# Slot arithmetic on GpSimd, scatters spread anew, and turned sums copied before the normalised rows, in a one-core Mamba-2 and mixture-of-experts kernel

## The chip, the core and the metric

The kernel runs on one core of a Trainium2 chip. The metric is the device time of one execution in microseconds (us); the kernel before has a median of 817.68 us over three runs (816.87 to 819.04). Engines are named as in the profile: PE is TensorE (PEld its weight loads), DVE is VectorE, ACT is ScalarE, POOL is GpSimd, SP is SyncE, which here only issues DMAs.

## The reference

16 sequences of 512 tokens with 128 channels pass through a Mamba-2 block and then through a top-2 mixture of 8 experts, each followed by a residual sum and a layer norm. Cut to what matters here:

```python
# block 1: projections, causal convolution of 4 taps, silu, state-space scan, gated RMS norm, output projection
h = dA_t * h + dt_t * x_t (outer) B_t ;  y = C_t . h + D * x_t
x = layernorm(x + (y * rsqrt(mean(y*y) + eps) * norm_w * silu(z)) @ Wout.T)
# block 2: router and experts
gates = sigmoid(u @ centroids.T)
topk_vals, topk_idx = top_k(gates, 2)
gates = mask(topk_vals) / sum(mask)
out = sum_e gates[e] * (gelu(u @ W1[e] + b1[e]) @ W2[e] + b2[e])
x = layernorm(x + out)
```

## The kernel before, in words

**First phase (about 0 to 478 us).** One slot of work per sequence, 16 in all, written out one after another. Sequence n is scanned in slot n, in four chunks of 128 tokens (c = 0 to 3). In the same slot sequence q = n + 1 is projected and convolved, sequence r = n - 1 is normalised and routed, and the rows of sequence n - 2 are scattered, sorted by expert, into a table in HBM (`sorted_rows`). Each engine has its own instruction list in a fixed order; semaphores tie them together. An instruction that waits holds back everything behind it on its engine. Nothing is scheduled at run time, so the order is the order of the code.

The names that matter:

- PE, chunk c: exponents of the next chunk (`exponents`, L420 to L425, into the bank `pl`), transposes of the chunk (L518, L520), product with the carried state (L524), a projection of q (L399), at c = 1 the turned sums of q (L412, `turn_parts`, into the bank `p4`), the masked product (L542), the carried part (L548), and the state product (L556), which needs `Xdd` from POOL and `Btok` from ACT. At the end of chunk 1 the rows of r are transposed (L566) into the same bank `p4`, so that this waits both until ACT has normalised the rows (`u_ready`) and until ACT has copied the turned sums out of it (`S_ready`).
- ACT, chunk 1: it normalises the four row blocks of r (L810), applies the first tap (L730, `acc`), copies the decays of q (L719, `cur`), copies the turned sums (L725, `S`, `keep_parts`), and then squares `yv` (L783). `uT` (L822) is the copy of the transposed rows.
- DVE: `Gm` (L1076) opens each slot. `take_ranks` (L1005 to L1009) reads the ranks of sequence n - 2 out of PSUM at the end of chunk 0. `place_rows` (L1017 to L1027) at the end of chunk 1 works out the row number of each token's two copies (`slot`), and writes their weight and token number into the last two columns of `rowA` and `rowB`.
- POOL: `Xdd` (L1379) and `decayed` (L1373) for the scan, `gt` (L1359, the gated output, once a chunk), two powers (`rstd` L1394, `rms` L1415), and eight indirect DMAs (L1366) which scatter the rows of sequence n - 2: A0 and A1 behind `gt` of chunk 1, A2 and A3 behind that of chunk 2, and B0 to B3 behind `rms` at the slot's end. The first instruction of the next slot on POOL is `Xdd` of its chunk 0, which so stands behind all four B scatters.

After slot 15 comes a tail: sequence 15 is normalised and routed, and POOL scatters sequences 14 and 15 (eight DMAs each), while DVE works out a table of 136 tiles.

**Second phase (about 478 to 770 us).** 136 tiles of 128 sorted rows go through the experts. **Third phase (to 815 us).** The two expert outputs of each token are added and normalised. Neither is touched by the change, except that they start when the last scatter has landed.

Of the kernel before, what the change touches and what calls it, by code (L numbers as in the profile page):

```python
# [52 lines left out]
POS_STEPS = 4  # L53
# [24 lines left out]
def build(nc, t, out):  # L78
    ctx = ExitStack()
    with ctx:  # L80
# [6 lines left out]
        def sem(name):  # L87
# [31 lines left out]
        token_id = sb("token_id", [P, NC])  # L119
# [42 lines left out]
        rowA = [sb(f"rowA{i}", [P, NC, ROW]) for i in range(2)]  # L162
        rowB = [sb(f"rowB{i}", [P, NC, ROW]) for i in range(2)]
# [11 lines left out]
        slotf = sb("slotf", [P, NC, 2])  # L175
# [34 lines left out]
              for big in (acc, xc[0]) for i in range(2)]  # L210
# [40 lines left out]
                     "slot_ready", "parts_ready", "split_step")  # L251
        (x1_ready, Gm_ready, M_ready, Xdt_ready, v_ready, yv_ready, state_ready, sp_step, a_ready,
         tap_done, conv_done, carried_ready, ln_step, ve_ready, shift_ready, u_ready, gate_step, chosen_ready,
         ms_ready, pos_step, rank_read, slot_ready, parts_ready, split_step) = [sem(n) for n in names_dve]
        names_pool = ("picks_made", "Xdd_ready", "decayed_ready", "g_ready", "rms_ready", "rstd_ready")
        (picks_made, Xdd_ready, decayed_ready, g_ready, rms_ready, rstd_ready) = [sem(n) for n in names_pool]
# [136 lines left out]
        def _(pe):  # L393
# [106 lines left out]
            def slot_pe(s, scan, project, route):  # L500
# [4 lines left out]
                for c in range(NC):  # L505
                    tok = slice(c * P, (c + 1) * P)
                    n = NC * s.n + c
                    if scan and (c + 1 < NC or project):
                        if not route and c == 0:
                            pe.wait_ge(v_ready, 2)  # L510
                        exponents(s if c + 1 < NC else q, (c + 1) % NC)
# [23 lines left out]
                    if scan:  # L535
# [140 lines left out]
        def _(act):  # L676
# [109 lines left out]
            def slot_act(s, scan, project, route):  # L786
# [4 lines left out]
                for c in range(NC):  # L791
# [94 lines left out]
        def _(dve):  # L886
# [124 lines left out]

            def place_rows(r):

                link = chain(pos_step, POS_STEPS * r.n + 1)
                dve.wait_ge(rank_read, r.n + 1)
                dve.wait_ge(rowB_ready, r.n + 1)
                dve.reciprocal(gsum[:, :], gsum[:, :])  # L1017
                link(dve.tensor_tensor(prow[:, :, :, :], picks[:, :, :, :],
                                       rows[:, :, :].unsqueeze(2).broadcast_to([P, NC, 2, E]), ALU.mult))
                link(dve.tensor_reduce(slotf[:, :, :], prow[:, :, :, :], AX_X, ALU.add))  # L1020
                for row, k in ((rowA, 0), (rowB, 1)):
                    dve.scalar_tensor_tensor(out=row[r.par][:, :, P + 1], in0=top[:, :, k], scalar=2.0,
                                             in1=gsum[:, :], op0=ALU.mult, op1=ALU.mult)
                    dve.tensor_scalar(row[r.par][:, :, P].bitcast(I32), token_id[:, :],
                                      float(TOKENS * k), None, ALU.add)
                link(dve.tensor_copy(slot[r.par][:, :, :], slotf[:, :, :]))
                dve.tensor_scalar(token_id[:, :], token_id[:, :], float(TOKS), None,  # L1027
                                  ALU.add).then_inc(slot_ready, 1)
# [27 lines left out]
            def slot_dve(s, scan, project, route):  # L1056
# [24 lines left out]
                for c in range(NC):  # L1081
# [50 lines left out]
                    if c == 1 and not (isinstance(s.n, int) and s.n < 2):  # L1132
                        place_rows(s.plus(-2))
# [9 lines left out]
                if route:  # L1143
# [4 lines left out]
                    wait_apart(dve, gate_step, gate + 2)  # L1148
                    for k in range(NC):
# [349 lines left out]
```

## Time and profile before

| | |
|---|---|
| median of three runs | 817.68 us (816.87 to 819.04) |
| the profiled execution | 816.69 us, of which the span is 814.9 us |
| busy in the span | PE 667.5, DVE 617.5, ACT 475.8, POOL 433.0 us |
| granted clock of PE in slots 1 to 15 | 1.00, full speed |

The page gives busy time by engine, then the span in 40 slices. The first 22 slices are the slots, with PE and DVE both at 8 to 9 tenths. PE busy counts modelled ends of pipelined matmuls, so two engines near 9 tenths say only that both are candidates; which of them waits for which is read from the chain of waits and from the timelines of single engines.

### The profile page before, as it was taken

What the parts mean: (1) busy time and instruction counts of PE and PEld (TensorE: products, weight loads), DVE (VectorE), ACT (ScalarE), POOL (GpSimd) and SP (SyncE); (2) the same over time, 40 slices, a digit from 0 to 9 for tenths busy, and PEclk for the clock granted to TensorE, in tenths of its full rate; (3) what the DMA queues carried; (4) which work ended last, traced back from release to release, by engine and by line L of the source; (5) the groups of instructions that cost most, each with busy time, mean ns of one, the idle gap of its engine ahead of it and who ended that gap; (6) DMA issues with size and microseconds to landing.
All of it is one profiled execution on the core that took longest, in us unless ns stands there. A gap on an engine that the chain in (4) does not pass through costs nothing.

```text
span 814.9 us, 21092 instructions
## 1 busy us (share of the span) xinstructions
PE 667.5 (82%) x5092; PEld 546.9 (67%) x5093; DVE 617.5 (76%) x2128; ACT 475.8 (58%) x1179; POOL 433.0 (53%) x498
## 2 busy tenths in 40 slices
PE   7969999888898898988987139999999999999300
PEld 5846666566665566655665129999999999999300
DVE  4398989889999899998896536666667666667485
ACT  3737766676766767667673115555555555556165
POOL 4023265656656566565756634555555555555464
PEclk9999999999999999999999559999999999999755
DMA  9160010111101111011100122222222222222496
GB/s 258 33 229 14 15 41 14 37 30 40 41 14 37 31 40 37 18 33 34 41 20 24 57 60 57 66 63 65 64 65 65 65 63 64 65 64 70 108 311 203
DMA packets 74801, 54.09 MB, mean 66 GB/s; under 512 B 9435, under 2 KB 70110, under 8 KB 74480
## 3 DMA queue, kind: packets, MB, share of 16 engines
q1 hardware_dynamic: 56400, 31.90, 14.9%
q0 software_dynamic: 8448, 16.93, 6.3%
q10 hardware_dynamic: 9888, 4.49, 2.0%
q8 instruction: 29, 0.48, 0.3%
q14 instruction: 36, 0.29, 0.1%
HBM read 31.11 MB, written 22.69 MB: 66 GB/s over the span
## 4 chain that ended last, share of the span: by engine, by line
PE 71%; issue 9%; ACT 7%; DVE 5%; POOL 3%; DMA 2%; ACTq 1%; SPq 1%; DVEq 0%; POOLq 0%
PE pl L633 16%; PE p L645 14%; PE pj L399 5%; PE p L585 4%; PE p L593 3%; PE p L542 3%; PE p L548 2%; PE pj L627 2%; ACT rowA L810 2%; ACT sz L872 2%; POOL sorted_rows L1366 2%; PE pj L407 2%; PE p L556 2%; PE p L496 2%; PE p L407 2%
## 5 line engine op out<-in xcount | busy, mean ns | idle before, releaser
L851 ACT ACTIVATE L<-pl,b_sb 128x128 f32<-128x128 f32 x544 | 155.4, 369 | 118.1 <-PE pl L633 118.1
L1428 POOL DMA_INDIRECT moe_rows<-yv,xs x136 | 145.7, 1072 | 140.5 <-DVE yv L1235 124.1
L633 PE MATMUL pl<-Btok,M 128*128 128x128 f32 x1088 | 151.7, 283 | 1.2 <-DVE M L1223 0.7
L924 DVE SCALAR_TENSOR_TENSOR acc<-pj,conv_w_sb,acc 128x511 f32<-128x511 f32 (+2 forms) x192 | 142.7, 743 | 4.0 <-ACT acc L730 1.1
L645 PE MATMUL p<-w,L 128*128 x1088 | 143.9, 275 | 1.3 <-ACT L L851 1.3
L633 PEld LDWEIGHTS pl<-Btok,M 128*128 128x128 f32 x1088 | 133.7, 193 | 4.3 <-DVE M L1223 1.4
L645 PEld LDWEIGHTS p<-w,L 128*128 128x128 f32 x1088 | 132.4, 192 | 1.8 <-issue 1.8
L1219 DVE COPY Btok<-pj 128x128 f32<-128x128 f32 x136 | 39.7, 292 | 78.2 <-PE pl L633 63.2
L1379 POOL TENSOR_TENSOR Xdd<-Xdt,cur 128x256 f32<-128x256 f32 x48 | 29.5, 615 | 88.0 <-DVE Xdt L1091 80.1
L1366 POOL DMA_INDIRECT sorted_rows<-rowA,slot x64 | 64.7, 1011 | 19.1 <-issue 17.0
L1366 POOL DMA_INDIRECT sorted_rows<-rowB,slot x64 | 62.7, 980 | 18.0 <-issue 18.0
L730 ACT ACTIVATE acc<-pj,conv_b_sb,conv_w_sb 128x512 f32<-128x512 f32 x64 | 49.5, 773 | 35.4 <-PE pj L399 35.3
L399 PE MATMUL pj<-xT,w_xbc 128*128 128x512 f32 x128 | 66.5, 601 | 0.0
L542 PEld LDWEIGHTS p<-M,Xdt 128*64 128x64 f32 x512 | 27.3, 136 | 52.5 <-issue 48.9
L627 PE MATMUL pj<-ident,xs 128*128 128x128 f32 x136 | 39.9, 294 | 23.3 <-DMA xs<-sorted_rows 20.8
L1223 DVE COPY M<-w 128x512 f32 x136 | 57.0, 419 | 0.0
L688 ACT ACTIVATE pl<-pl 128x512 f32<-128x512 f32 x64 | 37.3, 582 | 33.8 <-PE pl L425 33.2
L1359 POOL TENSOR_TENSOR gt<-yv,sz 128x256 f32<-128x256 f32 x64 | 47.0, 734 | 11.3 <-DVE yv L1117 10.6
L1235 DVE SCALAR_TENSOR_TENSOR yv<-yv,xs 128x128 f32<-128x128 f32 x136 | 47.8, 352 | 4.8
L1232 DVE TENSOR_TENSOR yv<-p,b2e_mem 128x128 f32<-128x128 f32 x136 | 39.5, 291 | 15.2 <-PE p L645 8.9
L542 PE MATMUL p<-M,Xdt 128*64 128x128 f32 x512 | 42.1, 284 | 9.5 <-issue 6.8
L998 DVE TENSOR_TENSOR M<-pl,Gm 128x512 f32<-128x512 f32 x64 | 43.8, 685 | 2.0 <-ACT pl L688 1.4
(204 smaller groups left out, 1341.7 us busy)
## 6 DMA issues: line engine op xcount, KB each, us to landing
xs<-sorted_rows SPq DMA_DIRECT2D x136, 65.0 KB, 1.8
xres<-in_x SPq DMA_DIRECT2D x16, 256.0 KB
w<-in_w SPq DMA_DIRECT2D x2, 2048.0 KB, 10.2
acc<-moe_rows SPq DMA_DIRECT2D x16, 256.0 KB, 4.2
xc<-moe_rows SPq DMA_DIRECT2D x16, 256.0 KB, 5.0
out<-sz ACTq DMA_DIRECT2D x16, 256.0 KB, 4.6
moe_rows<-yv,xs POOLq DMA_INDIRECT x136, 2.4
xc<-in_x SPq DMA_DIRECT2D x4, 256.0 KB, 5.1
```

Source lines behind the costliest of these rows:

```text
L399: pe.matmul(pj[k % 2][:, :], w_xbc[:, k * P:(k + 1) * P], xT[:, q.n, :], start=True, stop=True).then_inc(proj_psum, 1)
L542: mm = pe.matmul(p7[half, (h // 2) * P:(h // 2 + 1) * P], Xdt[c % 2][:, h * HD:(h + 1) * HD], M[c % 2][:, h, :], start=(h < 2), stop=(c == ...
L627: pe.transpose(pj[k % 2][:, 0:P], xs[k][:, 0:P], ident[:, :]).then_inc(sT_psum, 1)
L633: mm = pe.matmul(pl[k % 2][:, f * P:(f + 1) * P], w1e[k % 2][:, f * P:(f + 1) * P], sT[k % 2][:, :], start=True, stop=True)
L645: mm = pe.matmul(o[:, 0:P], hT[k % 2][:, f, :], w2[:, bass.ds(e, 1), f, :].rearrange("p e d -> p (e d)"), start=(f == 0), stop=(f == FB - 1))
L730: act.activation(acc[:, c, :], pj[c % 2][:, :], ACT.Identity, bias=conv_b[:, c:c + 1], scale=conv_w[:, c, TAPS - 1:TAPS]).then_inc(tap0_do ...
L851: act.activation(hT[k % 2][:, f, :], pl[k % 2][:, f * P:(f + 1) * P], ACT.Gelu, bias=b1[:, bass.ds(e * FB + f, 1)]).then_inc(hT_ready, 1)
L924: ins = dve.scalar_tensor_tensor(out=acc[:, k, j:TOKS], in0=pj[k % 2][:, 0:TOKS - j], scalar=conv_w[:, k, TAPS - 1 - j:TAPS - j], in1=acc[ ...
L1223: dve.tensor_copy(w1e[k % 2], w1[:, bass.ds(e, 1), :].rearrange("p e f -> p (e f)")).then_inc(w1e_ready, 1)
L1235: dve.scalar_tensor_tensor(out=ye[k % 4], in0=ye[k % 4], scalar=xs[k][:, P + 1:P + 2], in1=xs[k][:, 0:P], op0=ALU.mult, op1=ALU.add).then_ ...
L1366: pool.indirect_dma_start(out=sorted_rows[:, :], out_offset=bass.IndirectOffsetOnAxis(slot[q.par][:, c, k:k + 1], 0), in_=(rowA, rowB)[k][ ...
L1428: pool.indirect_dma_start(out=moe_rows[:, :], out_offset=bass.IndirectOffsetOnAxis(xs[k][:, P:P + 1].bitcast(I32), 0), in_=ye[k % 4], in_o ...
```

## The change

`place_rows` leaves DVE and is written again for POOL, for both copies of a row at once. `rowA` and `rowB` become the two halves of one tile `pair`, and `token_id` gets two sets of columns. The sum over the eight experts, one `tensor_reduce` on DVE, becomes three halving additions. The reciprocal of the gate sum stays on DVE, in `take_ranks`. On POOL the arithmetic stands behind `gt` of chunk 0. The eight scatters are laid out anew: A0 ahead of `Xdd` of chunk 2, A1 to A3 behind `gt` of chunk 1, B0 behind that of chunk 2, and B1 to B3 behind `rms`. On ACT the copy of the turned sums goes ahead of the normalising, and the copy of the decays goes to chunk 3. On PE the exponents of chunk 2 are issued ahead of the state product of chunk 0 and no longer at the start of chunk 1.

```diff
@@ take_ranks (DVE)
                 dve.wait_ge(rank_psum, r.n + 1)
+                wait(dve, slot_ready, r.n)
 ...
                 dve.tensor_tensor(next_row[:, :], p4[:, NC * E:(NC + 1) * E], next_row[:, :],
                                   ALU.add).then_inc(rank_read, 1)
+                dve.reciprocal(gsum[:, :], gsum[:, :]).then_inc(rows_ready, 1)
-            def place_rows(r):     (DVE, ten instructions, L1013 to L1028)
@@ slot_pe
-                    if scan and (c + 1 < NC or project):
+                    if scan and c != 1 and (c + 1 < NC or project):
 ...
                             pe.wait_ge(Btok_ready, (NC - 1) * s.n + c + 1)
                             pe.wait_ge(Xdd_ready, (NC - 1) * s.n + c + 1)
                             if c == 0:
+                                exponents(s, 2)
                                 pe.wait_ge(sz_ready, CC * (s.n + 1))
@@ slot_act
+                    if project and c == 1:
+                        keep_parts(q, p4[0:KS, 0:P])
                     if route and c == 1:
 ...
-                    if project and c == 1:
+                    if project and c == 3:
                         set_current(q)
-                        keep_parts(q, p4[0:KS, 0:P])
@@ gpsimd
+            def place_rows(r):
+                done = [PLACE_STEPS * r.n]
+                def link(ins):
+                    done[0] += 1
+                    ins.then_inc(place_step, 1)
+                    pool.wait_ge(place_step, done[0])
+                pool.wait_ge(rows_ready, r.n + 1)
+                wait(pool, slot_ready, r.n)
+                pool.wait_ge(rowB_ready, r.n + 1)
+                pool.tensor_tensor(gain[:, :], gsum[:, :], gsum[:, :], ALU.add)
+                link(pool.tensor_tensor(prow[:, :, :, :], picks[:, :, :, :],
+                                        rows[:, :, :].unsqueeze(2).broadcast_to([P, NC, 2, E]), ALU.mult))
+                part = prow
+                for k in range(3):
+                    w = E >> (k + 1)
+                    if k == 1:
+                        pool.tensor_tensor(pair[r.par][:, :, :, P + 1], top[:, :, 0:2].rearrange("p c k -> p k c"),
+                                           gain[:, :].unsqueeze(1).broadcast_to([P, 2, NC]), ALU.mult)
+                    if k == 2:
+                        pool.tensor_copy(pair[r.par][:, :, :, P].bitcast(I32), token_id[:, :, :])
+                    link(pool.tensor_tensor(half[k][:, :, :, :], part[:, :, :, 0:w], part[:, :, :, w:2 * w],
+                                            ALU.add))
+                    part = half[k]
+                link(pool.tensor_copy(slot[r.par][:, :, :], half[2][:, :, :, 0]))
+                pool.tensor_scalar(token_id[:, :, :], token_id[:, :, :], 1.0, float(TOKS), ALU.mult,
+                                   ALU.add).then_inc(slot_ready, 1)
```

On POOL, from the first instruction of a slot to the first of the next, with the kernel before (the names are those of the list above; `sorted_rows<-rowA` is a scatter of A):

```order
L1379 TENSOR_TENSOR Xdd<-Xdt,cur 128x256
L1394 TENSOR_TENSOR rstd<-ve,neg_half 128x4
L1373 TENSOR_TENSOR decayed<-state,cur 128x256
L1379 TENSOR_TENSOR Xdd<-Xdt,cur 128x256
L1359 TENSOR_TENSOR gt<-yv,sz 128x2x128
L1373 TENSOR_TENSOR decayed<-state,cur 128x256
L1379 TENSOR_TENSOR Xdd<-Xdt,cur 128x256
L1359 TENSOR_TENSOR gt<-yv,sz 128x2x128
L1366 DMA sorted_rows<-rowA,slot 67584x130 x2
L1359 TENSOR_TENSOR gt<-yv,sz 128x2x128
L1366 DMA sorted_rows<-rowA,slot 67584x130 x2
L1359 TENSOR_TENSOR gt<-yv,sz 128x2x128
```

And with the changed kernel, from the first `gt` of a slot on to the first instruction of the next:

```order
L1345 TENSOR_TENSOR gt<-yv,sz 128x2x128
L1360 TENSOR_TENSOR gain<-gsum 128x4
L1361 TENSOR_TENSOR prow<-picks,rows 128x64
L1371 TENSOR_TENSOR half<-prow 128x32
L1367 TENSOR_TENSOR pair<-top,gain 128x8
L1371 TENSOR_TENSOR half<-half 128x16
L1370 CAST pair<-token_id 128x8
L1371 TENSOR_TENSOR half<-half 128x8
L1374 CAST slot<-half 128x8
L1375 TENSOR_SCALAR token_id<-token_id 128x8
L1389 TENSOR_TENSOR decayed<-state,cur 128x256
L1382 DMA sorted_rows<-pair,slot 67584x130
```

Nine small instructions and one scatter now stand between `gt` of chunk 0 and `Xdd` of chunk 2, and three scatters, where there were four, between `rms` and the next slot.

On ACT, chunk 1 of a slot before, from the normalising to the copy of the transposed rows:

```order
L810 ACTIVATE rowA<-rowA,shift,rstd 128x128 x4
L730 ACTIVATE acc<-pj,conv_b_sb,conv_w_sb 128x512
L719 COPY cur<-vals 128x80
L725 CAST S<-p 96x128
L783 ACTIVATE ysq<-yv 128x2x128
L822 COPY uT<-p 128x512
```

And the same place now:

```order
L729 CAST S<-p 96x128
L816 ACTIVATE pair<-pair,shift,rstd 128x128 x4
L734 ACTIVATE acc<-pj,conv_b_sb,conv_w_sb 128x512
L787 ACTIVATE ysq<-yv 128x2x128
L827 COPY uT<-p 128x512
```

The copy `S` no longer stands behind the normalising and a tap, and `cur` is gone from this chunk.

On PE, chunk 0 and the head of chunk 1 now:

```order
L545 MATMUL p<-M,Xdt 64x128 x4
L423 MATMUL pl<-too_early,ident_b 128x512
L425 MATMUL pl<-pick_s,S 128x512
L428 MATMUL pl<-S,pick_t 128x128 x4
L560 MATMUL p<-Xdd,Btok 128x256
L521 MATMUL p<-ident,xc 128x128 x2
```

Before, the three rows of exponents stood behind the state product; both orders have them behind PE's wait for `Xdd`.

## Rows read from the trace of the kernel before

**Rows 1.** Busy time by engine in one steady slot (stretch, length, busy, clock).

```profile
288.00:314.00 26.00, 23.10 (x164) 15.93 (x162) 23.54 (x77) 17.53 (x35) 16.25 (x20) 1.00 0.11 33
```

**Rows 2.** The chain that ended last: start us, us, engine, tile, line, count.

```profile
299.43 1.32 issue
...
304.54 1.25 ACT rowA L810 x3
305.78 0.66 ACT acc L730
306.45 0.15 ACT cur L719
306.60 0.17 ACT S L725
306.76 0.14 issue
306.90 0.63 PE p L566 x4
...
323.42 0.86 PE pj L399 x2
```

**Rows 3.** Timeline of PE in the same slot, the state product of chunk 2.

```profile
310.88 0.60 PE L556 MATMUL p<-Xdd,Btok 128*128 128x256 f32 x2
```

**Rows 4.** Timeline of POOL in that slot: start us, us, what, [idle before].

```profile
299.04 0.96 POOL L1366 DMA_INDIRECT sorted_rows<-rowB,slot  x1 [0.30 <-issue]
300.03 0.62 POOL L1379 TENSOR_TENSOR Xdd<-Xdt,cur 128x256 f32<-128x256 f32 x1
...
304.04 0.73 POOL L1359 TENSOR_TENSOR gt<-yv,sz 128x256 f32<-128x256 f32 x1
...
309.58 0.61 POOL L1379 TENSOR_TENSOR Xdd<-Xdt,cur 128x256 f32<-128x256 f32 x1 [2.09 <-DVE Xdt L1091]
```

**Rows 5.** Timeline of DVE in that slot.

```profile
301.45 0.42 DVE L1122 COPY state<-p 128x256 f32<-128x256 f32 x1 [0.34 <-PE p L556]
...
303.63 0.46 DVE L1103 SCALAR_TENSOR_TENSOR shift<-mv,rstd 128x4 f32<-128x4 f32 x1
...
306.71 0.17 DVE L1017 RECIPROCAL gsum<-gsum 128x4 f32<-128x4 f32 x1
...
307.92 0.74 DVE L924 SCALAR_TENSOR_TENSOR acc<-pj,conv_w_sb,acc 128x511 f32<-128x511 f32 x1
```

**Rows 6.** Timeline of ACT in that slot, the copy of the transposed rows.

```profile
307.62 0.59 ACT L822 COPY uT<-p 128x512 f32<-128x512 f32 x1 [0.55 <-PE p L566]
```

**Rows 7.** All 16 `Gm` (min/median/max ns, first and last start), then those opening slots 2, 3.

```profile
L1076 DVE TENSOR_TENSOR Gm<-p,upto x16: 677/681/691, 38.5 to 424.9; 128x512 f32<-128x512 f32 x16
...
92.24 0.68 DVE L1076 TENSOR_TENSOR Gm<-p,upto 128x512 f32<-128x512 f32 x1
...
116.98 0.68 DVE L1076 TENSOR_TENSOR Gm<-p,upto 128x512 f32<-128x512 f32 x1
```

**Rows 8.** Timeline of POOL at the start, two small additions, the second waiting for the first.

```profile
6.19 0.21 POOL L1347 TENSOR_TENSOR which<-ident 96x16 f32<-96x16 f32 x1
6.48 0.22 POOL L1348 TENSOR_TENSOR which<-which,ident 96x16 f32<-96x16 f32 x1
```

**Rows 9.** The small `shift` on DVE: ns min/median/max over all slots.

```profile
L1103 DVE SCALAR_TENSOR_TENSOR shift<-mv,rstd x16: 161/463/465, 73.8 to 452.4; 128x4 f32<-128x4 f32 x16
```

**Rows 10.** Timelines of DVE and POOL in the tail.

```profile
449.66 0.32 DVE L1054 TENSOR_SCALAR ve<-mv 128x4 f32<-128x4 f32 x1
...
450.32 0.96 POOL L1366 DMA_INDIRECT sorted_rows<-rowB,slot  x1 [0.30 <-issue]
451.31 1.04 POOL L1394 TENSOR_TENSOR rstd<-ve,neg_half 128x4 f32<-128x4 f32 x1
454.49 1.03 POOL L1366 DMA_INDIRECT sorted_rows<-rowA,slot  x1 [2.14 <-DVE token_id L1027]
...
466.34 1.92 POOL L1366 DMA_INDIRECT sorted_rows<-rowA,slot  x1 [0.31 <-issue]
...
473.03 0.40 DVE L1207 CAST table<-tval 1x136 int32<-1x136 f32 x1
```

More of the change, by code:

```diff
@@ L52 @@
 NH = NC * H
-POS_STEPS = 4
+POS_STEPS = 1
+PLACE_STEPS = 5
 FIN_STEPS = 3
@@ L118, in build @@
         iota_tile = sb("iota_tile", [P, TILES])
-        token_id = sb("token_id", [P, NC])
+        token_id = sb("token_id", [P, 2, NC])
         region = sb("region", [P, E])
@@ L161, in build @@
         shift = sb("shift", [P, NC])
-        rowA = [sb(f"rowA{i}", [P, NC, ROW]) for i in range(2)]
-        rowB = [sb(f"rowB{i}", [P, NC, ROW]) for i in range(2)]
+        pair = [sb(f"pair{i}", [P, 2, NC, ROW]) for i in range(2)]
+        rowA = [b[:, 0] for b in pair]
+        rowB = [b[:, 1] for b in pair]
         uT = sb("uT", [P, TOKS])
@@ L174, in build @@
         prow = sb("prow", [P, NC, 2, E])
-        slotf = sb("slotf", [P, NC, 2])
+        half = [sb(f"half{i}", [P, NC, 2, E >> (i + 1)]) for i in range(3)]
+        gain = sb("gain", [P, NC])
         slot = [sb(f"slot{i}", [P, NC, 2], I32) for i in range(2)]
@@ L1010, in take_ranks @@
                                   ALU.add).then_inc(rank_read, 1)
[L1012 to L1028, printed above, removed]
+                dve.reciprocal(gsum[:, :], gsum[:, :]).then_inc(rows_ready, 1)
             def residual(s):
@@ L1131, in slot_dve @@
                         take_ranks(s.plus(-2))
-                    if c == 1 and not (isinstance(s.n, int) and s.n < 2):
-                        place_rows(s.plus(-2))
                 gate = GATE_STEPS * (r.n if route else 0)
@@ L1148, in slot_dve @@
                     wait_apart(dve, gate_step, gate + 2)
+                    wait(dve, slot_ready, r.n)
                     for k in range(NC):
@@ L1164, in slot_dve @@
                     link(dve.tensor_copy(topf[:, :, :], topi[:, :, 0:2]))
-                    wait(dve, slot_ready, r.n)
                     link(dve.tensor_tensor(
@@ L1175, in _ @@
             take_ranks(Seq(0, SEQS - 1))
-            place_rows(Seq(0, SEQS - 1))
             link = chain(table_step, 0)
@@ L1333, in _ @@
                            allow_small_or_imprecise_dtypes=True))
-            step(pool.iota(token_id[:, :], pattern=[[P, NC]], base=0, channel_multiplier=1,
+            step(pool.iota(token_id[:, :, :], pattern=[[TOKENS, 2], [P, NC]], base=0, channel_multiplier=1,
                            allow_small_or_imprecise_dtypes=True))
@@ L1398, in slot_pool @@
                     gate_y(s, 0)
+                if scatters:
+                    place_rows(old)
+                if scan:
                     decay_state(s, 2)
+                if scatters:
+                    scatter(old, 0, 0)
+                if scan:
                     decay_x(s, 2)
@@ L1402, in slot_pool @@
                 if scatters:
-                    scatter(old, 0, 0)
-                    scatter(old, 1, 0)
+                    for c in range(1, NC):
+                        scatter(old, c, 0)
                 if scan:
@@ L1407, in slot_pool @@
                 if scatters:
-                    scatter(old, 2, 0)
-                    scatter(old, 3, 0)
+                    scatter(old, 0, 1)
                 if scan:
@@ L1416, in slot_pool @@
                 if scatters:
-                    for c in range(NC):
+                    for c in range(1, NC):
                         scatter(old, c, 1)
             slots(pool, slot_pool)
+            place_rows(Seq(0, SEQS - 1))
             for k in range(2):
```

8 lines of the change are left out of this document (4 added, 4 removed).

## The prediction, made before the changed kernel had run

> **What bounds the kernel now.** I read first the busy time by stage, then the chain of waits through one steady slot, then the timelines of POOL, DVE and ACT beside it. In a steady slot PE is busy 23.1 and DVE 23.5 of 26 us, at a full granted clock [rows 1], so neither alone is the bound; the reader is to see that both have about 2.5 us to give and to ask which wait ends last. The chain answers: from 306.90 to past 323.42 it is PE without a gap, and before that it leaves PE twice [rows 2]. First PE stands 1.32 us behind its masked product until the state product of chunk 0. POOL explains that: `Xdd`, which the product needs, starts at 300.03, the moment the last of four B scatters ends [rows 4]. Second, the chain goes from the normalising on ACT through a tap, the `cur` copy and the `S` copy to the transposes at 306.90 [rows 2]. The transposes need the normalised rows, done at 305.78, but the copy `S` lets them go only 0.98 us later (0.66 + 0.15 + 0.17). The slots are regular: `Gm` of slot 3 starts at 116.98 and that of slot 15 at 424.9, twelve periods of 25.66 us; slot 2, which has no B scatters ahead of it, lasts 116.98 - 92.24 = 24.74 us [rows 7].
>
> **The `S` copy ahead of the normalising.** It takes 0.98 us out of the way to the transposes in every slot that both routes and projects: 1 to 14, fourteen. What is late next is the `uT` copy, which waited 0.55 us for those transposes [rows 6]; ACT reaches it 0.32 us earlier, since `cur` and `S` are gone ahead of it, so it can follow by 0.87, and the rest is taken up by PE, whose queue from there to the slot's end is full. I take 0.98, with 0.86 as the low end. 14 x 0.98 = 13.7 us. `cur` goes to chunk 3, beside PE work, and is needed only in the next slot: nothing. The price is a wait: ACT's normalising is now queued behind PE's turned sums. Estimate: the state ends at 301.5, then half a microsecond for the product with it, 0.86 for the projection [rows 2], 0.2 for the turn and 0.26 for the copy make 303.3, and `shift` ends at 303.6. So this costs nothing, but it is the thinnest margin on ACT.
>
> **One B scatter fewer behind `rms`.** A scatter costs POOL 1.26 us (0.96 and the 0.30 ahead of it, [rows 4]). `Xdd` could then start at 298.77, about when its input is there, and PE's 1.32 us go, less what the exponents do there: they are 0.66 us and move ahead of the state product, which is work that PE did just behind it, so the sum on PE is the same and the exponents reach ACT earlier. But PE is not alone there. DVE waited only 0.34 us for the state [rows 5]; from there its queue is full up to `shift`, on which ACT waits. So the slot gains what `shift` gains: 0.34, at most 0.50 with small waits behind it, less 0.09 for the added reciprocal. I take 0.40 in slots 3 to 14 (12 x 0.40 = 4.8) and 0.4 in slot 15, together 5.2 us. Ends: 0.25, and 0.92, the difference between the steady period and slot 2 [rows 7], which also holds an earlier start.
>
> **The arithmetic off DVE.** It took 307.92 - 306.71 = 1.21 us a slot [rows 5]. It lies behind `shift` and ahead of the wait of DVE for chunk 2, so it is not on the chain. I cost its removal at nothing: it only keeps DVE from becoming the bound once PE moves up by 1.4 us.
>
> **The arithmetic on POOL.** Nine instructions, five of them waited for. A 96x16 addition with a wait costs 6.48 - 6.19 = 0.29 us from start to start [rows 8]. Five x 0.29 = 1.43, 0.08 more for the 64 elements of the first product (0.62 us for 256 elements, [rows 4], is 1.7 ns an element), and four unwaited ones at about 0.15: 2.1 us. Ends: 1.2 us, DVE's price, and 9 x 0.62 = 5.6 us, the row of the large product. I take 2.1, nearest to the rows of like size. What lies behind it: `decayed` and A0, then `Xdd` of chunk 2, for which PE comes at 310.88 [rows 3], or about 309.4 with the gains above. `gt` ends at 304.77 - 0.45 = 304.3; then 2.1, a short wait for the state, 0.6 for `decayed`, 1.2 for A0 and 0.6 for `Xdd` make 309.2. So there is room for an arithmetic of about 2.5 us; each microsecond beyond it costs one in every slot from 2 on. Behind chunk 2 POOL issues four scatters up to the last `gt`, as before.
>
> The Trainium skill speaks against this step: GPSIMD Engine Reference, Engine selection, gives two-input elementwise work to VectorE, since GpSimd is about twice as slow. By that rule an estimate would be 2 x 1.21 = 2.4 us, still within the 2.5; no run so far shows these instructions on POOL, and the sum would stay the same by either.
>
> **The tail.** With three B scatters `rstd` waits no longer for POOL but for `ve`, whose row ends at 449.98: 450.1 instead of 451.31 [rows 10]. The 2.14 us in which POOL then waited for DVE's arithmetic become 2.2 us of its own, so A0 comes 1.15 us earlier. But the arithmetic for sequence 15, which DVE did beside the eight scatters, now stands between them and the next eight (466.34): 2.1 + 0.17 - 0.3 = 1.9. Net 0.8 us slower, with the gains of the slots in front. The 16 scatters themselves stay. DVE's tile table, whose last row ends at 473.43 [rows 10], starts when that arithmetic is done, some 4 us later, and is ready at 477.4; eight scatters of 1.26 behind the ninth's place at 467.1 end after that and must land first, so the table stays covered.
>
> **Sum.** 13.7 + 5.2 - 0.8 = 18.1 us off the profiled execution of 816.69, whose span is 814.9: 798.6. The median of the runs shown is 0.99 above it; from 817.68 it gives 799.6, and I say 799.5. The second and third phase are untouched. With both low ends it is 14 x 0.86 + 13 x 0.25 - 0.8 = 14.5 off, 803; with the state product's high end 13 x 0.52 more, 793. A difference under 0.3% (2.5 us) can't be told from none here.
>
> **Rivals.** (1) The arithmetic on POOL takes 2.6 to 3.7 us, say 3.1. For it: short rows and strides of 130 elements that no row of before shows. Against: the same engine's small rows at 0.21. Then 0.6 us of each of 13 slots goes back, and 2 x 1.0 in the tail: 10 less, 809.5.
> (2) Slower: POOL's small instructions are held up by DVE. `shift`, a 128x4 instruction, takes 0.161 us in the tail and 0.463 in the slots, beside POOL's work [rows 9]: the two hold each other up by 0.30. If each of the nine is held so, the arithmetic is 2.1 + 2.7 = 4.8 us, 2.3 beyond the room, against a gain of 1.38 a slot: 0.9 lost in each of 12 slots, about 1.3 in slot 2, 1 in slot 15, 0.8 + 5.4 in the tail, less 1 in slot 1: 18 us slower, 836. It decides from an arithmetic of 3.7 us on, price and room together. Against it: DVE's work in that stretch is taps, `yv` and state sums that read PSUM, and POOL's large products cost the same in every slot. That the two share their way to SBUF stands also in the Trainium skill, GPSIMD Engine Reference, Specifications, for DVE instructions with two SBUF inputs; the rows of `shift` agree, and by that rule the taps with their one SBUF input would not hold POOL.
> (3) The copy `S` becomes the wait: the turned sums come later than `shift`, and normalising starts 0.5 us late. For it: 0.3 us of margin. Against: PE is ahead there, as its 1.32 us are gone. 18.1 - 14 x 0.5 = 11 off, 806.5.
> (4) Nothing moves since DVE is full in truth: 817. Against: DVE did wait, 0.34 us for the state [rows 5].
>
> **How the numbers follow.** Forecast 0.70, (1) 0.12, (2) 0.08, (3) 0.07, (4) 0.03. The forecast's own range is 793 to 803; with (1) and (3) the range reaches 793.5 to 811, and leaves out (2), (4) and a rest. Faster: 0.70 + 0.12 + 0.07 less a little for a long arithmetic, 0.87; same 0.04; slower 0.09.
>
> **What would show it.** A period between two `Gm` of 24.2 to 24.4 us; the state product of chunk 0 within 0.2 us of the masked product, not counting the exponents; the transposes of rows waiting for `rowA` and no longer for `S`, some 0.45 us behind the state product of chunk 1; nine POOL instructions from the first `gt` in 2.0 to 2.4 us; in the tail, 2.1 us of arithmetic between the eighth and ninth scatter. The prediction is wrong if the state product of chunk 2 waits for `Xdd`, if the arithmetic is over 2.5 us, or if `shift` has not moved up in the slot.

## The result, and the profile after

The changed kernel took 797.24 us (median of 4, 795.83 to 798.2) against 817.27 us of the kernel before beside it: a ratio of 0.9751, 95% interval 0.9728 to 0.9773. Forecast were 799.5 us and a range of 793.5 to 811. The profiled execution took 798.2 us.

I read it in the order of the prediction. First the `Gm` that open the slots: all of them (min/median/max ns, first and last start), then two single ones (start us, us).

```profile
L1065 DVE TENSOR_TENSOR Gm<-p,upto x16: 679/681/692, 38.0 to 404.1; 128x512 f32<-128x512 f32 x16
...
91.51 0.68 DVE L1065 TENSOR_TENSOR Gm<-p,upto 128x512 f32<-128x512 f32 x1
...
115.40 0.68 DVE L1065 TENSOR_TENSOR Gm<-p,upto 128x512 f32<-128x512 f32 x1
```

The period is (404.1 - 115.4) / 12 = 24.06 us against 25.66 [rows 7]: 1.60 us less in each of twelve slots. Slot 2 lasts 23.89 against 24.74, and slot 1, where no B scatter lies behind `rms` either, has lost the same 0.85. Busy time in a steady slot (stretch, length, busy of PE, weight load, DVE, ACT, POOL, clock, DMA share, GB/s):

```profile
284.00:308.00 24.00, 22.91 (x162) 15.90 (x161) 21.99 (x68) 17.41 (x34) 17.77 (x28) 1.00 0.11 34
```

PE does nearly the same work in 24 us instead of 26 [rows 1]. The two stretches are not the same share of a period, so I take DVE and POOL over slots 3 to 14 as a whole: DVE is busy 263.5 us instead of 278.6 and POOL 213.1 instead of 190.5, that is 1.3 us less and 1.9 us more a slot. The timeline of PE in the slot whose `Gm` starts at 283.86 (start us, us, what, [idle before]):

```profile
286.32 0.66 PE L545 MATMUL p<-M,Xdt 128*64 128x128 f32 x8
287.02 0.38 PE L423 MATMUL pl<-too_early,ident_b 128*128 128x512 bf16 x1
...
287.68 0.65 PE L560 MATMUL p<-Xdd,Btok 128*128 128x256 f32 x2
...
289.05 0.70 PE L527 MATMUL p<-state,xc 128*128 128x256 f32 x2 [0.40 <-DVE state L1111]
...
291.73 0.60 PE L560 MATMUL p<-Xdd,Btok 128*128 128x256 f32 x2
292.87 0.66 PE L570 MATMUL p<-ident,pair 128*128 128x128 f32 x4 [0.54 <-ACT pair L816]
```

PE's 1.32 us ahead of the state product of chunk 0 [rows 2] are gone: L560 follows the exponents without a wait. The transposes (L570) now wait for the normalised rows, 0.54 us behind the state product of chunk 1. ACT in the same slot:

```profile
290.70 0.26 ACT L729 CAST S<-p 96x128 bf16<-96x128 f32 x1 [1.74 <-PE p L415]
291.17 1.65 ACT L816 ACTIVATE pair<-pair,shift,rstd 128x128 f32<-128x128 f32 x4 [0.20 <-DVE shift L1092]
...
293.69 0.56 ACT L827 COPY uT<-p 128x512 f32<-128x512 f32 x1
```

The `S` copy stands ahead of the normalising and is done 0.2 us before `shift` comes; the last to come is `shift`. DVE from the state to the third chunk:

```profile
288.58 0.41 DVE L1111 COPY state<-p 128x256 f32<-128x256 f32 x1
...
290.67 0.47 DVE L1092 SCALAR_TENSOR_TENSOR shift<-mv,rstd 128x4 f32<-128x4 f32 x1
...
293.75 0.74 DVE L929 SCALAR_TENSOR_TENSOR acc<-pj,conv_w_sb,acc 128x511 f32<-128x511 f32 x1
295.08 0.42 DVE L1080 TENSOR_TENSOR Xdt<-p,cur 128x256 f32<-128x256 f32 x1 [0.58 <-PE p L523]
```

The state waits for nothing (0.34 before, [rows 5]). `shift` ends 7.28 us behind `Gm` in this slot; in the median of slots 3 to 14 it is 7.35 against 7.86 before, 0.51 earlier. In the same median the transposes start 9.09 us behind `Gm` instead of 10.66, so nearly the whole gain of the slot is made by there. Without the arithmetic DVE waits 0.58 us for chunk 2. POOL:

```profile
285.32 0.96 POOL L1382 DMA_INDIRECT sorted_rows<-pair,slot  x1 [0.30 <-issue]
286.31 0.61 POOL L1395 TENSOR_TENSOR Xdd<-Xdt,cur 128x256 f32<-128x256 f32 x1
...
291.76 0.20 POOL L1360 TENSOR_TENSOR gain<-gsum 128x4 f32<-128x4 f32 x1
291.91 0.33 POOL L1361 TENSOR_TENSOR prow<-picks,rows 128x64 f32<-128x64 f32 x1
292.31 0.25 POOL L1371 TENSOR_TENSOR half<-prow 128x32 f32<-128x32 f32 x1
292.64 0.21 POOL L1367 TENSOR_TENSOR pair<-top,gain 128x8 f32<-128x8 f32 x1
...
293.77 0.19 POOL L1375 TENSOR_SCALAR token_id<-token_id 128x8 f32<-128x8 f32 x1
293.94 0.60 POOL L1389 TENSOR_TENSOR decayed<-state,cur 128x256 f32<-128x256 f32 x1
```

The nine small instructions take 293.94 - 291.76 = 2.18 us. In the tail, behind the last slot:

```profile
428.16 1.04 POOL L1410 TENSOR_TENSOR rstd<-ve,neg_half 128x4 f32<-128x4 f32 x1 [0.16 <-DVE ve L1043]
429.19 0.19 POOL L1360 TENSOR_TENSOR gain<-gsum 128x4 f32<-128x4 f32 x1
...
432.18 1.09 POOL L1382 DMA_INDIRECT sorted_rows<-pair,slot  x1 [0.79 <-POOL token_id L1375]
...
443.76 0.21 POOL L1360 TENSOR_TENSOR gain<-gsum 128x4 f32<-128x4 f32 x1
...
446.75 1.06 POOL L1382 DMA_INDIRECT sorted_rows<-pair,slot  x1 [0.78 <-POOL token_id L1375]
...
456.30 0.95 POOL L1382 DMA_INDIRECT sorted_rows<-pair,slot  x1 [0.30 <-issue]
```

From the last `Gm` to the last scatter's start it is 52.2 us, 0.9 more than the 51.3 before. Of the second and third phase, whose code is the same, I count the time from that start to the end of the span: 796.3 - 456.3 = 340.0, before 338.7.

### The profile page after: what moved, and what is told of

Read it like the earlier page. It is cut to its first block, busy times and chain, and to the rows that moved or that the text cites. A ratio compares the mean times of both kernels' runs of the same rounds, so it can differ in the third digit from the quotient of the medians.

```text
span 796.3 us, 21108 instructions
## 1 busy us (share of the span) xinstructions
PE 673.3 (85%) x5092; PEld 548.5 (69%) x5093; DVE 600.1 (75%) x2000; ACT 473.8 (60%) x1179; POOL 465.2 (58%) x642
## 4 chain that ended last, share of the span: by engine, by line
PE 69%; DVE 9%; issue 8%; POOL 5%; ACT 4%; DMA 3%; DVEq 1%; SPq 0%; ACTq 0%; POOLq 0%
PE pl L637 16%; PE p L649 15%; PE pj L402 4%; PE p L589 4%; PE p L597 3%; POOL sorted_rows L1382 3%; PE p L551 2%; PE pj L631 2%; PE p L545 2%; ACT pair L816 2%; PE pj L410 2%; PE p L499 2%; PE p L527 2%; PE p L410 2%; PE pl L446 2%
## 5 line engine op out<-in xcount | busy, mean ns | idle before, releaser
L1450 POOL DMA_INDIRECT moe_rows<-yv,xs x136 | 147.3, 1083 | 139.4 <-DVE yv L1221 122.0
L1382 POOL DMA_INDIRECT sorted_rows<-pair,slot x128 | 128.3, 1002 | 35.2 <-issue 33.6
L734 ACT ACTIVATE acc<-pj,conv_b_sb,conv_w_sb 128x512 f32<-128x512 f32 x64 | 49.5, 773 | 33.1 <-PE pj L402 33.1
L1080 DVE TENSOR_TENSOR Xdt<-p,cur 128x256 f32<-128x256 f32 x64 | 27.0, 422 | 20.5 <-ACT Btok L802 10.4
```

The source lines that it names most:

```text
L734: act.activation(acc[:, c, :], pj[c % 2][:, :], ACT.Identity, bias=conv_b[:, c:c + 1], scale=conv_w[:, c, TAPS - 1:TAPS]).then_inc(tap0_do ...
L1382: pool.indirect_dma_start(out=sorted_rows[:, :], out_offset=bass.IndirectOffsetOnAxis(slot[q.par][:, c, k:k + 1], 0), in_=(rowA, rowB)[k][ ...
L1450: pool.indirect_dma_start(out=moe_rows[:, :], out_offset=bass.IndirectOffsetOnAxis(xs[k][:, P:P + 1].bitcast(I32), 0), in_=ye[k % 4], in_o ...
```

## The experiments

The theory at this point: a slot hangs on the chain from the state of chunk 0 over `shift`, the normalising and the transposes to the pairs' end; the copies and the scatter each took their own term off it, and DVE's arithmetic lay beside it at no price. The rivals: the gain is DVE's relief, or the exponents' new place. In the table the period is that of slots 3 to 14, "tail" runs from the last `Gm` to the last scatter's start, and the ratio is to the kernel before on the same chip.

| kernel | median us | ratio, 95% | period | tail |
|---|---|---|---|---|
| changed | 797.24 | 0.9751, 0.9728 to 0.9773 | 24.06 | 52.2 |
| e1_copies_back | 811.85 | 0.9932, 0.9915 to 0.9949 | 25.09 | 52.2 |
| e2_four_behind | 813.52 | 0.9954, 0.9936 to 0.9971 | 25.12 | 56.2 |
| e3_exponents_back | 800.7 | 0.9772, 0.975 to 0.9794 | 24.13 | 52.4 |
| e4_dve_load | 806.21 | 0.985, 0.9827 to 0.9874 | 24.69 | 52.5 |
| e5_four_more | 813.57 | 0.9944, 0.9923 to 0.9965 | 25.03 | 55.6 |
| b1_copies_ahead | 810.0 | 0.9893, 0.9868 to 0.9917 | 25.02 | 51.3 |
| b2_three_behind | 813.13 | 0.9922, 0.9898 to 0.9945 | 25.28 | 49.9 |
| b3_both | 806.09 | 0.9836, 0.9812 to 0.9859 | 24.75 | 50.1 |
| t1_tail_on_dve | 791.23 | 0.9698, 0.9684 to 0.9712 | 24.06 | 47.7 |
| v1_shift_early | 793.99 | 0.9726, 0.9708 to 0.9743 | 23.70 | 52.2 |
| v2_all | 790.69 | 0.9681, 0.9667 to 0.9694 | 23.82 | 49.5 |
| v3_early_and_tail | 795.59 | 0.9684, 0.9665 to 0.9703 | 23.94 | 48.0 |

**Undo the copies** (e1, from the changed kernel: `S` and `cur` copied in chunk 1 behind the normalising, as before):

```diff
-                    if project and c == 1:
-                        keep_parts(q, p4[0:KS, 0:P])
...
-                    if project and c == 3:
+                    if project and c == 1:
...
+                        keep_parts(q, p4[0:KS, 0:P])
```

> The changed kernel with ACT's two copies (turned sums, decays) back behind the normalising and the tap of chunk 1. Theory: the copy of the turned sums was on the path to the transposes of the rows; that path takes back 0.86 us (what slots 1 and 2 gained) to 1.07 us in each of 14 slots: 12 to 15 us, so 809 to 812 us, period of a slot 24.9 to 25.1 us, and the transposes wait for S again. Rival (the relief of DVE carries the gain, the copy only filled a gap): at most 3 us slower, about 800.

Measured: 811.85 us, period 25.09, so 1.03 us a slot. PE in the slot whose `Gm` starts at 267.25:

```profile
277.39 0.63 PE L570 MATMUL p<-ident,pair 128*128 128x128 f32 x4 [1.60 <-ACT S L729]
```

And ACT there:

```profile
274.63 1.65 ACT L814 ACTIVATE pair<-pair,shift,rstd 128x128 f32<-128x128 f32 x4 [2.20 <-DVE shift L1091]
...
276.99 0.26 ACT L729 CAST S<-p 96x128 bf16<-96x128 f32 x1
```

The rows are done at 276.28 and `S` at 277.25, and the transposes start right behind `S`: the 0.98 of the prediction, in the place it named.

**Undo the scatter's move** (e2, all four B scatters behind `rms`):

```diff
-                if scatters:
-                    scatter(old, 0, 1)
...
-                    for c in range(1, NC):
+                    for c in range(NC):
```

> The changed kernel with scatter B0 back behind rms, so that four scatters again stand ahead of Xdd of chunk 0. Theory: Xdd comes 1.26 us later, PE waits, and since the exponents now stand between that wait and the state product, the state comes 1.0 us later, shift too, in slots 3 to 15; the tail adds 1.2: 13 to 15 us slower, 810 to 812, period 25.0 to 25.1. Rival (the stall was beside other work, as DVE waited only 0.34 us for it in the kernel before): 4 to 6 us slower, 802.

Measured: 813.52 us, period 25.12 (1.06 a slot); PE of the slot whose `Gm` starts at 265.58:

```profile
270.10 0.38 PE L423 MATMUL pl<-too_early,ident_b 128*128 128x512 bf16 x1 [1.32 <-issue]
...
270.75 0.65 PE L560 MATMUL p<-Xdd,Btok 128*128 128x256 f32 x2
```

PE's 1.32 us are back, now ahead of the exponents that stand there. The state product starts 5.17 us behind `Gm`, 0.66 later than in the kernel before (4.51): the exponents now lie between the wait and the product. That is why undoing this move here costs more than the move alone gives (b2, below). The tail grew by 4.0 us where I expected 1.2; in slot 15, too, everything behind the fourth scatter comes later.

**The exponents alone** (e3, those of chunk 2 back in their old place):

```diff
-                    if scan and c != 1 and (c + 1 < NC or project):
+                    if scan and (c + 1 < NC or project):
...
-                                exponents(s, 2)
```

> The changed kernel with the exponents of chunk 2 back at the start of chunk 1, behind the state product. Theory: PE does the same work in the other order, DVE does not wait for the state either way and ACT has 0.9 us to spare: no change, 796 to 799, period 24.0 to 24.1. Rival (the earlier exponents are what brought shift forward by 0.59 where I had reckoned 0.40): 0.2 us a slot, 3 us slower, 800.

The period is 24.13, 0.07 a slot, and the last scatter starts at 456.1 (456.3 in the changed kernel). So the exponents' place gives next to nothing. The median is 3.5 us higher, but the intervals of the two ratios overlap, and the kernel before took 819.03 us beside this one and 817.27 beside the changed kernel. What shows of the rest lies behind the last scatter: 345.1 us to the end of the span instead of 340.0, in code that is the same. PE there waits once for long:

```profile
710.42 2.08 PE L636 MATMUL pl<-Btok,M 128*128 128x128 f32 x8 [2.28 <-DVE M L1208]
```

b3 below has the same wait, 2.26 us, and 343.1 us behind its last scatter's start. Hence the slots are compared by their periods below, not by the medians.

**Give DVE its load back** (e4: nine small DVE instructions whose results nobody uses, where the arithmetic stood):

```diff
+                for k in range(3):
+                    dve.tensor_scalar(idle_a[:, :], iota_tile[:, 0:8], 1.0, None, ALU.add)
+                    dve.tensor_scalar(idle_b[:, :], iota_tile[:, 0:8], 1.0, None, ALU.add)
+                    link(dve.tensor_scalar(idle_c[:, :], iota_tile[:, 0:64], 1.0, None, ALU.add))
...
+                    if c == 1 and not (isinstance(s.n, int) and s.n < 2):
+                        idle_work(s.n - 2)
```

> The changed kernel with nine added DVE instructions of no use (about 1.2 us, as long as the arithmetic that left DVE) where that arithmetic stood. Theory: DVE waits 0.58 us there for the transposes, so chunk 2's Xdt comes 0.55 us later and its masked product 0.4 us later, in 13 or 14 slots: 5 to 6 us slower, 802 to 803, period 24.4 to 24.5. Rival (DVE became free by the whole 1.2 us, it is the bound): 16 us slower, 813. Rival (the prediction's own cost of nothing): 797.

Measured: 806.21 us, period 24.69. DVE in the slot whose `Gm` starts at 264.43:

```profile
274.39 0.16 DVE L1027 TENSOR_SCALAR idle_a<-iota_tile 128x8 f32<-128x8 f32 x1
...
274.77 0.47 DVE L1027 TENSOR_SCALAR idle_a<-iota_tile 128x8 f32<-128x8 f32 x1
...
275.82 0.75 DVE L933 SCALAR_TENSOR_TENSOR acc<-pj,conv_w_sb,acc 128x511 f32<-128x511 f32 x1
276.49 0.42 DVE L1092 TENSOR_TENSOR Xdt<-p,cur 128x256 f32<-128x256 f32 x1
```

And PE there, the masked product of chunk 2:

```profile
277.01 0.66 PE L549 MATMUL p<-M,Xdt 128*64 128x128 f32 x8 [0.56 <-issue]
```

DVE no longer waits for chunk 2, PE stands 0.56 us ahead of its product until `Xdt` is there, and `Xdt` starts 12.06 us behind `Gm` instead of 11.29. The load is 275.82 - 274.39 = 1.43 us and the slot pays 0.63 of it, more than I expected. The 0.58 us in which the changed kernel's DVE waits here cover the rest, or nearly: 1.43 - 0.58 = 0.85, of which `Xdt` shows 0.77. The load is longer than what had left DVE, which is 1.21 less the 0.09 of the reciprocal, or 1.12 us; so 0.63 is more than the price of the arithmetic itself. But DVE's work at this place is not free.

**More arithmetic on POOL** (e5: four waited-for additions whose result nobody uses, ahead of the step that releases the scatters):

```diff
+                link(pool.tensor_tensor(filler[:, :], gain[:, :], gain[:, :], ALU.add))
...
```

> The changed kernel with four more waited-for 128x4 additions in POOL's arithmetic, about 1.1 us (2.2 becomes 3.3). Theory: there is room for 2.5; beyond it the state product of chunk 2 waits for Xdd: 0.8 us in each of 13 slots and 2.2 in the tail, 12 to 14 us slower, 810, period 24.85. Rival (POOL is off the path): only the tail, 2 us slower, 799.

Measured: 813.57 us, period 25.03. The four cost 1.12 us, 0.28 from start to start. PE in the slot whose `Gm` starts at 267.41:

```profile
281.41 0.67 PE L561 MATMUL p<-Xdd,Btok 128*128 128x256 f32 x2 [0.74 <-POOL Xdd L1400]
```

The state product of chunk 2 now waits for `Xdd`, as rival (1) says of a long arithmetic. Of 1.12 us more the slot pays 0.97, so the room ends at some 2.18 + 0.15 = 2.3 us of arithmetic; I had 2.5. The tail grew by 3.4 us, 1.1 more than twice the four.

**One move alone, in the kernel before** (b1 only the copies, b2 only the scatter, b3 both; the arithmetic stays on DVE and the exponents where they were). The edits:

```diff
+                    if project and c == 1:
+                        keep_parts(q, p4[0:KS, 0:P])
...
+                    scatter(old, 0, 1)
...
-                    for c in range(NC):
+                    for c in range(1, NC):
```

> The kernel before with nothing changed but ACT's two copies: the turned sums ahead of the normalising, the decays in chunk 3. Theory: 0.86 to 0.98 us less in each of 14 slots, 12 to 14 us faster, 803 to 805, period 24.7 to 24.8. Rival (with DVE still carrying the arithmetic it is full and nothing moves): within 3 us of the kernel before.

> The kernel before with nothing changed but scatter B0, issued ahead of the last gt and no longer behind rms. Theory: PE's wait of 1.32 us goes, the slot gains 0.4 to 0.6 (what DVE waited for the state, and its followers) in 12 slots, 0.4 in slot 15 and 1.1 in the tail: 6 to 9 us faster, 808 to 811, period 25.1 to 25.3. Rival (all of PE's 1.32 us is gained): 17 us faster, 800. Rival (gt of chunk 3 and the gated output come later by the scatter's 1.2 us and eat it): no change.

> The kernel before with both moves (copies ahead on ACT, B0 ahead of the last gt), the arithmetic still on DVE and the exponents of chunk 2 in their old place. Theory: the two gains add up, less 0.3 to 0.5 us a slot because DVE's 1.2 us of arithmetic now reach past its wait in chunk 2; period 24.3 to 24.5, and the tail is 3 us shorter than in the changed kernel: 798 to 801, that is within 4 us of the changed kernel. Rival (the move of the arithmetic is what made room, without it DVE is the bound): period 25.1 or more, 810.

Periods: b1 25.02 (0.64 off), b2 25.28 (0.38 off, my 0.40), b3 24.75 (0.91 off). b1 fell short of its 0.98 and b3 of its sum. For b1 the timeline of DVE (`Gm` at 265.82) says why:

```profile
277.42 0.17 DVE L1028 TENSOR_SCALAR token_id<-token_id 128x4 f32<-128x4 f32 x1
277.50 0.74 DVE L925 SCALAR_TENSOR_TENSOR acc<-pj,conv_w_sb,acc 128x511 f32<-128x511 f32 x1
278.16 0.41 DVE L1092 TENSOR_TENSOR Xdt<-p,cur 128x256 f32<-128x256 f32 x1
```

Before, DVE waited 0.42 us ahead of this `Xdt` of chunk 2. In b1 the wait is gone: DVE, full with the arithmetic, sets when chunk 2 starts. Its `Xdt` comes 12.34 us behind `Gm` instead of 12.84 in the kernel before, whatever PE has gained. In b2 DVE still waits 0.42 us there.

Where each gain goes is read from the same instructions of PE in all slots. The table has their starts in us behind `Gm`, medians of slots 3 to 14 ("output" is the product of `gt` with `w_out`, L593 before and L597 now):

| kernel | transposes | masked product, chunk 2 | output | next `Gm` |
|---|---|---|---|---|
| before | 10.66 | 13.51 | 22.33 | 25.61 |
| b1 | 9.60 | 12.86 | 21.69 | 24.97 |
| b2 | 10.16 | 13.00 | 21.92 | 25.25 |
| b3 | 9.08 | 12.34 | 21.40 | 24.73 |
| changed | 9.09 | 11.96 | 20.79 | 24.06 |
| e4 | 9.08 | 12.58 | 21.41 | 24.68 |

With both moves the transposes are as early as in the changed kernel, 1.58 us earlier than before. Then b3 gives back 0.38 at the masked product, where PE waits for DVE's `Xdt`, and 0.23 more at the output, where it waits for the last `gt` on POOL. In b3, in the slot whose `Gm` starts at 264.97, two lines of PE and then one of POOL:

```profile
277.32 0.66 PE L542 MATMUL p<-M,Xdt 128*64 128x128 f32 x8 [0.32 <-issue]
...
286.37 2.05 PE L593 MATMUL p<-w_out,gt 128*128 128x128 f32 x16
...
285.57 0.75 POOL L1360 TENSOR_TENSOR gt<-yv,sz 128x256 f32<-128x256 f32 x1
```

The last `gt` ends at 286.32 and the output starts at 286.37. Between the `gt` of chunk 1 and the last one b3 has five scatters and the changed kernel four, since A0 stands ahead of chunk 2 there. In the changed kernel (`Gm` at 259.73) the last `gt` ends a microsecond ahead of the output:

```profile
278.81 0.73 POOL L1345 TENSOR_TENSOR gt<-yv,sz 128x256 f32<-128x256 f32 x1
...
280.51 1.98 PE L597 MATMUL p<-w_out,gt 128*128 128x128 f32 x16
```

In e4 nothing but DVE's load differs from the changed kernel, and all of its 0.62 arises at the masked product.

**The tail's arithmetic on DVE** (t1: in the changed kernel, for sequences 14 and 15 only, whose arithmetic lies outside the slots):

```diff
+            def place_rows(r):
...
+                link(dve.tensor_reduce(half[0][:, :, :, 0], prow[:, :, :, :], AX_X, ALU.add))
...
+                        if not scan:
+                            place_rows(s.plus(-2))
...
+            place_rows(Seq(0, SEQS - 1))
...
-                if scatters:
+                if scatters and scan:
...
-            place_rows(Seq(0, SEQS - 1))
```

> The changed kernel, with the place arithmetic of the last two sequences (which lie in the tail, outside the slots) back on VectorE. If the tail's terms were read rightly, the two arithmetics (about 2.0 us each on GpSimd ahead of the first and ninth scatter) go beside other work: the first costs 1.2 us on VectorE instead of 2.0, the second lies beside the first eight scatters, and the wait of 0.79 us ahead of the ninth scatter goes. From the fifteenth mask to the last scatter 47.5 to 49 us instead of 52.2, and 793 to 794 in all, 3 to 4.5 below the changed kernel. The period of the slots stays at 24.06. Rival: VectorE, which has the table to build beside the scatters, is late with it by the same time, and nothing is gained: 797.

Measured: 791.23 us; the tail is 47.7 instead of 52.2 and the period the same. The slots and the tail want the arithmetic on different engines: in a slot DVE is full, in the tail POOL is.

**`shift` a step earlier** (v1, from the changed kernel; DVE: `shift` ahead of `carried` of chunk 1, the tap behind both and the mask; ACT: `S` behind the normalising, ahead of the tap):

```diff
-                    if project and c > 0:
+                    if project and c > 0 and not (scan and c == 1):
...
+                    if project and scan and c == 1:
+                        tap(q, c - 1, 1)
```

> The changed kernel, with `shift` a step earlier in the slot: on VectorE it stands ahead of `carried` of chunk 1, and the first tap of chunk 1 stands behind it; on ScalarE the copy of the turned sums stands behind the row's normalising. In the profile of the changed kernel the normalising waits for `shift`, which ends last. If the slot hangs on that chain, `shift` comes 0.5 to 0.8 us earlier, and the period falls from 24.06 to 23.4 to 23.6: 788 to 791 for the whole. If VectorE is as full as the experiment with the added VectorE work says (0.63 of 1.4 us paid), moving its work within the slot gains only part: period 23.7 to 23.9, 792 to 795. If the state product waits for `carried` instead, nothing is gained or the slots get longer: 797 to 803.

Measured: 793.99 us, period 23.70. The small `shift` over all slots (ns min/median/max):

```profile
L1087 DVE SCALAR_TENSOR_TENSOR shift<-mv,rstd x16: 153/153/164, 72.8 to 424.1; 128x4 f32<-128x4 f32 x16
```

ACT in the slot whose `Gm` starts at 256.7, the normalising:

```profile
262.79 1.65 ACT L814 ACTIVATE pair<-pair,shift,rstd 128x128 f32<-128x128 f32 x4 [0.91 <-DVE shift L1087]
```

PE there, the state product of chunk 1, the transposes and the state product of chunk 2:

```profile
264.65 0.60 PE L560 MATMUL p<-Xdd,Btok 128*128 128x256 f32 x2
265.08 0.60 PE L570 MATMUL p<-ident,pair 128*128 128x128 f32 x4
...
269.36 0.67 PE L560 MATMUL p<-Xdd,Btok 128*128 128x256 f32 x2
```

And POOL:

```profile
268.59 0.62 POOL L1397 TENSOR_TENSOR Xdd<-Xdt,cur 128x256 f32<-128x256 f32 x1
```

`shift` ends 1.30 us earlier in the slot, since it has moved and is no longer held up by 0.30, and PE's wait ahead of the transposes is gone. The slot gains 0.36 of what the transposes gain, which is 0.71 (they start 8.38 us behind `Gm` instead of 9.09, medians). Of the three expectations the middle one held. `Xdd` of chunk 2 now ends at 269.21, 0.15 us before the product that needs it (0.37 in the median of the changed kernel). In e5 and v2, where the profile shows PE waiting for `Xdd`, the product also starts 0.14 to 0.15 us behind its end, so here too POOL sets the product's start. Of the 0.71 some 0.15 is lost there and just behind it, and 0.20 ahead of it, where DVE's state of chunk 1 ends at 266.61 and PE's product with it starts at 266.67.

**All together** (v2: both, and the first A scatter ahead of the decayed state of chunk 2; v3: both without that move):

```diff
-                if scan:
-                    decay_state(s, 2)
...
+                if scan:
+                    decay_state(s, 2)
```

> Both of the above together, and the first A scatter of a slot ahead of the decayed state of chunk 2 on GpSimd. The gains add, as one lies in the slots and one in the tail: 784 to 788. If the slots gain nothing, 793 to 794 from the tail alone. Rival: the decayed state, now behind a scatter of 1.2 us, becomes what chunk 2 waits for, and each slot costs 0.3 more: 790 to 795.

> The version with `shift` early and the tail's arithmetic on VectorE, without the move of the A scatter. With that move the period was 23.82 us instead of 23.70, and the stretch behind the fifteenth mask 49.5 instead of the 47.7 of the kernel with the tail's arithmetic on VectorE, since in the last slot the decayed state of chunk 2 came behind a scatter. If that is what it cost, this version has a period of 23.70, 47.7 us behind the fifteenth mask and the last scatter at 446.6, and takes 786 to 788. Rival: the early `shift` and VectorE's arithmetic themselves get in each other's way in the last slots; then it is 789 to 791, as with the move.

v2 took 790.69 us: the scatter's move cost 0.12 in each slot and more in the last one, where PE shows the wait:

```profile
412.28 0.83 PE L560 MATMUL p<-Xdd,Btok 128*128 128x256 f32 x2 [0.96 <-POOL Xdd L1417]
```

v3 should have had the better of it and did not: a ratio of 0.9684 like v2's 0.9681, 795.59 us beside 821.3 of the kernel before. In the other series that kernel took 816.27 to 819.03 us, so part of the high median is not this version's. Its profile has three odd pieces, all in code that another kernel has too: the period is 23.94 where v1's is 23.70, with two waits a slot longer by 0.11 to 0.13 each; the time behind the last scatter's start is 344.9, with a wait of PE of 2.37 us as in e3; and SP's queue of pad rows, which took 4.12 us in the changed kernel, took 13.12:

```profile
440.55 13.12 SPq L323 DMA_DIRECT2D sorted_rows<-pad_tile  x4
```

It ends at 453.7, behind the last scatter's start at 450.46, and the chain that ended last runs through it. The cause of the three stays open: whether the chip or the place of the code makes them was not tried. t1, v1, v2 and v3 all beat the changed kernel by point, and t1, v2 and v3 with intervals that do not touch the changed kernel's. Among those three the intervals overlap, and none is shown to be the best.

## Why the prediction was right, and where it was not

- **The sum.** Up to the last scatter the profile is 476.2 - 456.3 = 19.9 us shorter; 18.1 were forecast. It splits into 12 x 1.60 = 19.2 in the steady slots, 1.7 in slots 1 and 2, 0.9 given back in the tail and 0.1 in slot 0. The second and third phase took 1.3 us more in this execution; the medians lie 20.0 apart.
- **The `S` copy ahead.** The place was right: b1 moves the transposes by 1.06, where 0.98 was forecast, and e1 pays 1.03 a slot for undoing it. In slots 1 and 2 it gave 0.85, the low end. Rival (3) is refuted: `S` waited 1.74 us for PE and still ended before `shift`.
- **One B scatter fewer.** `shift` came 0.51 us earlier instead of 0.40, and b2 moves the transposes by 0.50; of that the period keeps 0.38, as 0.1 is lost again at the output. PE's 1.32 us went and mostly did not become time, as said. Undone in the changed kernel it costs 1.06, since the exponents then stand behind the wait (e2).
- **The arithmetic off DVE: the step that failed.** "I cost its removal at nothing." With the arithmetic still on DVE the two moves give the transposes all they can, 1.58 us (b3), where 1.38 was forecast; but at chunk 2 DVE comes last and takes 0.38 back. DVE had 0.42 us of waiting there, and the copies alone take 1.06 off PE's way: in b1 0.65 of it arrives at the masked product. e4 shows the same place the other way round, 0.63 for a load of 1.43 us. The prediction named this role ("keeps DVE from becoming the bound") and then put the whole gain down to the two moves. Some 12 x 0.38 = 4.6 us of the result belong to this step. The rest of the difference between b3 and the changed kernel (0.69 in all) arises at the last `gt` and behind it, and goes with the scatters' new layout, though no run moves A0 alone, and the exponents' place, 0.07 in e3, may have a part in it. With the two moves and nothing else a slot gains 0.91 and not 1.38. The forecast of the whole came out since the whole change also has the relief of DVE and the early A0; for the term that was put at nothing this is luck and no proof.
- **The arithmetic on POOL.** 2.18 us against 2.1, each instruction 0.19 to 0.33 us. Rivals (1) and (2) are refuted for it; e5 shows that (1) had its mechanism and nearly its threshold right.
- **The tail.** +0.9 us against a net +0.4 (0.8 for the tail, less 0.4 in slot 15), and the near miss hides two larger ones. Each arithmetic cost POOL 0.8 us more than forecast, 0.62 of it because the first scatter behind it starts 0.79 us behind the last small instruction and not 0.17. Against that, `rstd` came 2.28 us earlier behind the last `Gm` (24.10 instead of 26.38) where 1.6 were forecast (1.2 in the tail and 0.4 in slot 15), and from the ninth scatter to the last it took 0.34 less. t1 shows what the stay on POOL costs there: 4.5 us.
- **Rival (4)**, DVE full in truth, was wrong for the whole and right for a part: with the arithmetic on DVE it has no wait at chunk 2 any more once the copies are moved (b1, b3); with the scatter's move alone it keeps it (b2).

## What to carry to other kernels

An edit that frees an engine beside the critical path can be worth a quarter of the gain together with the edits that shorten the path (0.38 of 1.60 us here; alone it was not run): compare the gain per period with that engine's waits at the same place in the order before costing it at nothing. Undoing a part and adding it alone give different prices (1.03 and 0.64 for the copies here); both are needed to say what it is worth, and the starts of a few fixed instructions behind the slot's first show where each part of a gain is lost again. Work may want one engine in the steady loop and another in the tail, and where code outside the change varies by up to 6.8 us, a period read from the trace tells more than the median.

## What the runs showed of the hardware

- A 128x4 or 128x8 instruction costs 0.19 to 0.21 us on POOL and 0.28 from start to start where the next waits for it; the arithmetic is 2.18 us on POOL. On DVE it was 1.21 with the reciprocal [rows 5], 1.12 without; the same results cost DVE 1.02 in t1 (427.66 to 428.68), with one reduction where POOL has three additions. That is a factor of about 2.
- A small DVE instruction was held up from 0.15 to 0.46 us while POOL ran a 128x256 product: `shift` at its old place [rows 9], beside `Xdd`, and in e4 one of the nine, with a single input tensor, beside the decayed state (299.46 to 299.93, POOL 299.28 to 299.89). `shift` was not held when moved to where POOL stands still (v1: 153 ns in the median). Nothing like it shows on POOL's side, whose small instructions take as long in the slots as in the tail.
- A scatter that follows its last input's instruction directly starts 0.78 to 0.80 us behind that one's end (in the tail, in v2 in the slots, and in t1, where DVE wrote the input). With the decayed state between them it starts 0.21 us behind that, again 0.80 behind its input (293.96 to 294.76). So 0.6 us of this time can be covered by other work.
- The same second and third phase took from 338.3 us (t1) to 345.1 us (e3) from the last scatter's start to the end. Two pieces show: a single wait of PE for DVE's mask of 2.3 us about 250 us in, which e3, b3 and v3 have and the changed kernel has not; and PE's clock, which was 0.50 while PE stood still and came back at different moments after work resumed. From 10 to 15 us behind the last scatter's start it was 1.00 in the changed kernel and 0.50 in e3, that is 2.4 and 1.2 GHz. What decides on either was not tried.
